# Scaling expert outputs by the gate column directly, and moving the residual sum to the head of VectorE's step, in a gated attention and mixture-of-experts block

## The chip, the cores and the metric

One core of a Trainium2 chip runs the whole block. The metric is the device time of one launch in microseconds (us), the median of several runs. One execution was also taken by the hardware profiler; its trace gives every row shown here. TensorE is written PE (its weight loads PEld), VectorE DVE, ScalarE ACT, GpSimd POOL, and the DMA-issuing SyncE SP.

## The reference, cut to what matters

```python
# x: (128, 64, 128), 16 heads of 64, 8 experts, top 2
x = x + tanh(g_xattn) * xattn(layernorm(x), ctx, ctx, mask, Wq, Wk, Wv, Wo)
# the feed-forward half, on n = 8192 tokens
xf = layernorm(x);  logits = xf @ Wg + bg;  probs = softmax(logits)
w, idx = top_k(probs, 2);  w = w / sum(w)
comb = sum(one_hot(idx, 8) * w[..., None], axis=1)          # (n, 8), two non-zero weights
h = relu(einsum('nd,edh->enh', xf, W1) + b1)
y = einsum('enh,ehd->end', h, W2) + b2
x = x + tanh(g_ffn) * einsum('end,ne->nd', y, comb)
```

Every expert is computed for every token, and the routing weights (zero for six of eight experts) scale its output.

## The kernel before, in words

The 128 sequences of 64 tokens are cut into 16 groups of 8 sequences (512 tokens). Each engine runs one written-out program over 163 steps `s`; a group spans 8 steps, and `i = s % 8` is the place in the group. There is no scheduler: what orders the engines is this list and the semaphores. In one step of the steady state the attention of one sequence is advanced at several stages, two heads of the next group's queries are projected, and one expert is computed for a group that is two groups behind (`FFN_LAG` is 16 steps). Matmuls are done in three half-precision passes (lines L46 to L48), so for each result ScalarE writes a high half and VectorE or GpSimd the low half.

Two of the eight PSUM banks hold scores. The other six are handed out in turn by `take_bank`: each TensorE block takes the next bank and waits until what was in it six takes ago has been read. In a steady step TensorE takes banks for queries, values, queries, transposed probabilities (`PT`, L310), first half of the hidden layer (`hid`), attention output (`PV`), second half of `hid`, in odd steps the output projection `Wo`, and the expert output `y`. So in an even step the first `hid` block takes the bank of the previous step's `Wo` (free when VectorE has made the residual sum, L720), and the `PV` block the bank of the previous `y` (free when VectorE has scaled it, L704). With the router's extra bank taken at i=0, the first `hid` block of i=1 takes the bank of `y`.

VectorE's step in order: scale `y` into `y_scaled` (L704), the low half of the transposed normalised tokens at i=7 (L662), in even steps the residual sum (L720) for one pair of sequences, then other low halves, softmax sums and maxima, and at the end the router's small operations. At i=0 these are L816 to L828 (`logit`, `above`, `same`, `logit_max`, `expo`), at i=1 L831 to L851: `rank`, `picked`, `picked_sum`, `picked_inv`, `weight3` (L845) and `comb` (L851). `weight3` holds the routing weights three times, for the bias matmul; `comb` holds them once, multiplied by `out_scale[:, 1]`, which is tanh of the feed-forward gate over the square of the number by which the weights were enlarged. `y_scaled` is `y * comb`; GpSimd adds it to `x2` (L922), and VectorE does so for the last 14 (L748).

Of the kernel before, what the change touches and what calls it, by code (L numbers as in the profile page):

```python
# [16 lines left out]
P = 128  # L17
# [33 lines left out]
def flamingo_block(nc, x, ctx, mask, g_xattn, g_ffn, Wq, Wk, Wv, Wo, Wg, bg, W1, b1, W2, b2, out):  # L51
    stack = ExitStack()
    with stack:
# [3 lines left out]
        def sem(name):  # L57
            return stack.enter_context(nc.semaphore(name))
# [52 lines left out]
        weight3 = sb("weight3", [P, GT, 3, QUAD])  # L111
        picked_sum = sb("picked_sum", [P, GT])
        picked_inv = sb("picked_inv", [P, GT])
        comb = sb("comb", [P, 2, GT, E])
        pickedT = sb("pickedT", [STACK, N], F16)
        hid = sb("hid", [P, NR, N])
        hidH, hidL = (sb(f"hid{p}", [P, 2, HC, N], F16) for p in "HL")
# [2 lines left out]
        def as_f32(tensor, pattern):  # L120
# [49 lines left out]
        s_marked, s_mask_in = sem("score_banks_marked"), sem("mask_in_bank")  # L170
        s_ln = [{k: sem(f"ln{w}_{k}") for k in ("stats", "aggr", "var", "minus", "shift", "rows")} for w in range(2)]
        s_logit_in, s_gt, s_eq, s_gmax, s_gshift = (sem(n) for n in ("logit_in", "gt", "eq", "gate_max", "gate_shift"))
        s_rank, s_picked, s_psum, s_pinv, s_comb1, s_comb, s_pickT_low = (
            sem(n) for n in ("rank", "picked", "picked_sum", "picked_inv", "comb1", "comb", "pickedT_low"))

        s_zero, s_ident, s_one, s_tri, s_half, s_vzero, s_w3zero, s_b2zero = (
            sem(n) for n in ("ident_zero", "ident", "tri_one", "tri", "minus_half", "v_zero", "weight3_zero", "b2_zero"))
# [81 lines left out]
        def _(pe):  # L259
# [133 lines left out]
            for s in range(FIRST, LAST):  # L393
                g, i = s // GB, s % GB
                sooner = 2 if s < 0 else 0
                eg, ei = (s - FFN_LAG) // GB, (s - FFN_LAG) % GB
                hg, hi = (s - 1 - FFN_LAG) // GB, (s - 1 - FFN_LAG) % GB
                if within(g + 1, GROUPS):
                    queries(g + 1, 2 * i)
                if within(s // 2, TILES):  # L400
                    values(s // 2, s % 2)
                if within(g + 1, GROUPS):
                    queries(g + 1, 2 * i + 1)
                if within(s, B):
                    scores(s)
                if within(s - 2, B):
                    transpose_probs(s - 2)
                if within(eg, GROUPS):
                    hidden(eg, ei, 0)
                if within(s - 3, B):  # L410
                    probs_values(s - 3)
                if within(eg, GROUPS):
                    hidden(eg, ei, 1)
                if s % 2 == 1 and within((s - 5) // 2, TILES):
                    project_out((s - 5) // 2)
                if within(hg, GROUPS):
                    expert_out(hg, hi)
                if i == 6 and within(g + 2, GROUPS):
                    transposes("xT", g + 2, xhat, (s_ln[0]["rows"], g + 3), s_xT)
                if i == 6 - sooner and within(g + 1, GROUPS):  # L420
                    transposes("ctxT", g + 1, ctx_raw[:, (g + 1) % 2], ctx_loaded(g + 1), s_ctxT)
                if i == 6 and within(g - 1, GROUPS):
                    transposes("x2T", g - 1, x2hat, (s_ln[1]["rows"], g), s_x2T)
                if i == 0 and within(g - 2, GROUPS):
                    for freed in take_bank("logit", g - 2):
                        pe.wait_ge(*freed)
                    pe.wait_ge(s_x2T_low, g - 1)
                    for t in range(GT):
                        lhs = [c[:, g % 2, t * P:(t + 1) * P] for c in (x2tH, x2tL)]
                        last = three_passes(pe, bk("logit", g - 2)[:, t * E:(t + 1) * E], lhs, (wgH[:, :], wgL[:, :]))  # L430
                    last.then_inc(s_logit, 1)
                if i == 2 and within(g - 2, GROUPS):
                    for freed in take_bank("pickedT", g - 2):
                        pe.wait_ge(*freed)
                    pe.wait_ge(s_comb1, g - 1)
                    for t in range(GT):
                        last = pe.transpose(bk("pickedT", g - 2)[0:STACK, t * P:(t + 1) * P],
                                            weight3[:, t, :, :].rearrange("p n e -> p (n e)"), ident[:, :])
                    last.then_inc(s_pickT, 1)
                if i == 3 and within(g - 2, GROUPS):  # L440
                    for freed in take_bank("b2 out", g - 2):
                        pe.wait_ge(*freed)
                    pe.wait_ge(s_pickT_low, g - 1)
                    for t in range(GT):
                        cols = slice(t * P, (t + 1) * P)
                        last = pe.matmul(bk("b2 out", g - 2)[:, t * D:(t + 1) * D], pickedT[:, cols], b2_halves[:, :],
                                         start=True, stop=True)
                    last.then_inc(s_b2, 1)
# [185 lines left out]
        def _(dve):  # L634
# [53 lines left out]
            for s in range(FIRST, LAST):  # L688
# [3 lines left out]
                was_sooner = 2 if s - 1 < 0 else 0  # L692
                eg, ei = (s - FFN_LAG) // GB, (s - FFN_LAG) % GB
                yg, yi = (s - 2 - FFN_LAG) // GB, (s - 2 - FFN_LAG) % GB
                if within(yg, GROUPS):
                    m = yg * E + yi
                    if yi == 0:
                        dve.wait_ge(s_comb, yg + 1)
                    if m == 0:
                        dve.wait_ge(s_wdve, H // 4 + 10)  # L700
                    if m >= 2:
                        dve.wait_ge(*y_added(m - 2))
                    dve.wait_ge(s_y, m + 1)
                    dve.tensor_tensor(y_scaled[:, m % 2], bk("y", yg, yi)[:, :].rearrange("p (t d) -> p t d", t=GT),  # L704
                                      comb[:, yg % 2, :, yi].unsqueeze(2).to_broadcast([P, GT, D]),
                                      ALU.mult).then_inc(s_scaled, 1)
                if ph == 6 and within(pg - 1, GROUPS):
                    transposed_low("x2T", pg - 1, x2tL[:, (pg - 1) % 2, :], x2tH[:, (pg - 1) % 2, :], s_x2T_high, s_x2T_low)
                if s % 2 == 0 and within((s - 6) // 2, TILES):
                    t = (s - 6) // 2  # L710
                    rg, ri = t // GT, t % GT
                    if t == 0:
                        dve.wait_ge(s_scale, 1)
                        dve.wait_ge(s_wdve, H // 4 + 10)
                    if ri == 0 and rg >= NX2:
                        dve.wait_ge(s_store[(rg - NX2) % 2], 16 * ((rg - NX2) // 2 + 1))
                    if ri == 0:
                        dve.wait_ge(*x_loaded(rg))
                    dve.wait_ge(s_wo, t + 1)
                    dve.scalar_tensor_tensor(x2[:, rg % NX2, ri, :], bk("Wo", t)[:, 0:D], out_scale[:, 0:1],  # L720
                                             x_raw[:, rg % NX, ri, :], ALU.mult, ALU.add).then_inc(s_res, 1)
                if ph == 6 and within(pg + 2, GROUPS):
                    transposed_low("xT", pg + 2, xtL[:, pg % 2, :], xtH[:, pg % 2, :], s_xT_high, s_xT_low)
                if ph == 6 - was_sooner and within(pg + 1, GROUPS):
# [104 lines left out]
                if i == 1 and within(g - 2, GROUPS):  # L829
                    dve.wait_ge(s_above, g - 1)  # L830
                    dve.tensor_reduce(rank[:, :, :], above[:, :, :, :], AX.X, ALU.add).then_inc(s_rank, 1)  # L831
                    dve.wait_ge(s_rank, g - 1)
                    dve.wait_ge(s_gate_exp, g - 1)
                    if g >= 3:
                        dve.wait_ge(s_pickT, g - 2)
                    dve.scalar_tensor_tensor(picked[:, :, :], rank[:, :, :], 1.5, expo[:, g % 2], ALU.is_lt,
                                             ALU.mult).then_inc(s_picked, 1)
                    dve.wait_ge(s_picked, g - 1)
                    dve.tensor_reduce(picked_sum[:, :], picked[:, :, :], AX.X, ALU.add).then_inc(s_psum, 1)
                    dve.wait_ge(s_psum, g - 1)  # L840
                    dve.reciprocal(picked_inv[:, :], picked_sum[:, :]).then_inc(s_pinv, 1)
                    dve.wait_ge(s_pinv, g - 1)
                    if g == 2:
                        dve.wait_ge(s_w3zero, 1)
                    dve.tensor_tensor(weight3[:, :, :, 0:E], picked[:, :, :].unsqueeze(2).to_broadcast([P, GT, 3, E]),  # L845
                                      picked_inv[:, :].unsqueeze(2).unsqueeze(3).to_broadcast([P, GT, 3, E]),
                                      ALU.mult).then_inc(s_comb1, 1)
                    dve.wait_ge(s_comb1, g - 1)
                    if g >= 4:
                        dve.wait_ge(s_scaled, E * (g - 3))  # L850
                    dve.tensor_scalar(comb[:, g % 2], weight3[:, :, 0, 0:E], out_scale[:, 1:2], None,  # L851
                                      ALU.mult).then_inc(s_comb, 1)
                if i == 2 and within(g - 2, GROUPS):
                    dve.wait_ge(s_pickT_high, g - 1)
# [207 lines left out]
```

## Time and profile before

| | us |
|---|---|
| median of 3 runs (1050.44 to 1051.08) | 1050.65 |
| the profiled execution's own time | 1048.99 |
| its span, first to last instruction | 1047.3 |
| PE busy | 980.3 (94%) |
| ACT busy | 931.9 (89%) |
| DVE busy | 858.6 (82%) |
| POOL busy | 814.6 (78%) |

Busy shares are means over the whole span, and matmuls overlap in the pipe. What sets the time in a stretch is read from who waits for whom there, and from the start-to-start distance of TensorE's blocks.

### The profile page before, as it was taken

To read this page: it belongs to the slowest core of one execution; us is meant where nothing else is said; L and a number is where in the kernel's file an instruction comes from. 1 tells how busy PE (TensorE), PEld (TensorE's weight loads), DVE (VectorE), ACT (ScalarE), POOL (GpSimd) and SP (SyncE) were. 2 spreads that over 40 slices of the span, in tenths; PEclk is the share of its full clock that TensorE was granted. 3 is DMA by queue.
4 is the path that set the end of the run, shared out by engine and by line. 5 is a ranking of instruction groups with operands and counts; after the bars stand their busy time and mean duration, and the time that the engine had idled before them with its cause. 6 is when DMAs were issued, how large, how long until landed. Compare 5 with 4: busy or idle time off the path is not lost.

```text
span 1047.3 us, 36218 instructions
## 1 busy us (share of the span) xinstructions
PE 980.3 (94%) x13749; PEld 730.3 (70%) x13749; DVE 858.6 (82%) x1741; ACT 931.9 (89%) x1793; POOL 814.6 (78%) x817
## 2 busy tenths in 40 slices
PE   6878799999999999999999999999999999999886
PEld 4456567777777777777777777777777777777654
DVE  3587688897988889798888979888897988888777
ACT  3899899999898999989899998989999898989765
POOL 3587768778888877888887788888778888889942
PEclk9999899999999999999999999999999999999999
DMA  9134232323223232322333232232323222222100
GB/s 231 29 55 73 52 59 46 58 47 65 50 42 60 55 58 47 65 50 42 57 57 60 45 65 50 43 60 54 61 44 65 50 32 51 44 42 53 33 2 22
DMA packets 319803, 56.91 MB, mean 54 GB/s; under 512 B 288744, under 2 KB 319504, under 8 KB 319632
## 3 DMA queue, kind: packets, MB, share of 16 engines
q1 hardware_dynamic: 319632, 54.59, 27.9%
q8 instruction: 112, 1.84, 0.7%
q14 instruction: 59, 0.48, 0.2%
HBM read 16.81 MB, written 4.19 MB: 20 GB/s over the span
## 4 chain that ended last, share of the span: by engine, by line
PE 55%; POOL 12%; ACT 12%; DVE 10%; issue 9%; DMA 1%; ACTq 0%; POOLq 0%; SPq 0%; DVEq 0%
PE bank L46 17%; PE bank L48 16%; PE bank L47 16%; POOL hidL L888 3%; POOL rstd L869 3%; PE bank L310 3%; PE bank L265 2%; POOL ptL L927 2%; ACT bank L518 2%; ACT vH L558 2%; ACT pt L578 2%; DVE above L824 2%; DVE comb L851 1%; ACT qH L462 1%; POOL prob L933 1%
## 5 line engine op out<-in xcount | busy, mean ns | idle before, releaser
L888 POOL TENSOR_TENSOR hidL<-hid,hidH 128x512 f16<-128x512 f32 x242 | 277.6, 1163 | 17.6 <-ACT hidH L492 17.6
L927 POOL TENSOR_TENSOR ptL<-pt,ptH 128x512 f16<-128x512 f32 x128 | 149.4, 1167 | 104.7 <-ACT pt L578 104.7
L482 ACT ACTIVATE hid<-bank,b1col 128x512 f32<-128x512 f32 x256 | 189.0, 738 | 8.2 <-PE bank L48 8.1
L492 ACT ACTIVATE hidH<-bank,b1col 128x512 f16<-128x512 f32 x256 | 191.8, 749 | 0.0
L46 PE MATMUL bank<-w2H,hidH 128*128 128x128 f16 x1024 | 178.0, 219 | 13.3 <-POOL hidL L888 7.4
L657 DVE TENSOR_TENSOR qL<-bank,qH 128x512 f16<-128x512 f32 x224 | 153.4, 685 | 40.6 <-ACT qH L462 37.2
L462 ACT ACTIVATE qH<-bank 128x512 f16<-128x512 f32 x256 | 159.3, 626 | 28.2 <-PE bank L48 27.3
L48 PE MATMUL bank<-w2H,hidL 128*128 128x128 f16 x1024 | 178.1, 219 | 0.0
L47 PE MATMUL bank<-w2L,hidH 128*128 128x128 f16 x1024 | 178.1, 219 | 0.0
L922 POOL TENSOR_TENSOR x<-x,y_scaled 128x512 f32<-128x512 f32 x114 | 146.0, 1281 | 12.8 <-DVE x L731 12.8
L933 POOL TENSOR_TENSOR prob<-prob,row_inv 128x512 f32<-128x512 f32 x128 | 133.7, 1044 | 15.5 <-DVE row_inv L767 15.5
L704 DVE TENSOR_TENSOR y_scaled<-bank,comb 128x512 f32<-128x512 f32 x128 | 87.6, 684 | 58.6 <-PE bank L48 57.6
L46 PEld LDWEIGHTS bank<-w2H,hidH 128*128 128x128 f16 x1024 | 100.1, 98 | 27.0 <-issue 19.4
L46 PE MATMUL bank<-x2tH,w1H 128*128 128x512 f16 x256 | 97.4, 381 | 13.4 <-DVE x L720 11.3
L47 PEld LDWEIGHTS bank<-w2L,hidH 128*128 128x128 f16 x1024 | 100.1, 98 | 6.8
L46 PE MATMUL bank<-ctH,qH 128*128 128x64 f16 x1024 | 103.0, 193 | 0.6 <-ACT bank L518 0.6
L46 PEld LDWEIGHTS bank<-ctH,qH 128*128 128x128 f16 x1024 | 92.3, 98 | 16.0 <-ACT bank L518 1.0
L46 PE MATMUL bank<-ptH,vdH 128*128 128x64 f16 x1024 | 103.0, 193 | 0.3 <-issue 0.3
L48 PE MATMUL bank<-ptH,vdL 128*128 128x64 f16 x1024 | 103.2, 193 | 0.0
L47 PE MATMUL bank<-ptL,vdH 128*128 128x64 f16 x1024 | 103.2, 193 | 0.0
L48 PE MATMUL bank<-ctH,qL 128*128 128x64 f16 x1024 | 103.1, 193 | 0.0
L47 PE MATMUL bank<-ctL,qH 128*128 128x64 f16 x1024 | 103.1, 193 | 0.0
(139 smaller groups left out, 3527.3 us busy)
## 6 DMA issues: line engine op xcount, KB each, us to landing
vdH<-vH SPq DMA_DIRECT2D x256, 64.0 KB, 2.3
vdL<-vL SPq DMA_DIRECT2D x256, 64.0 KB, 2.3
x_raw<-in_x SPq DMA_DIRECT2D x16, 256.0 KB, 3.1
ctx_raw<-in_ctx SPq DMA_DIRECT2D x16, 256.0 KB, 3.1
mask_raw<-in_fside_Bx1xSxS SPq DMA_DIRECT2D x32, 128.0 KB, 2.8
out_x<-x SPq DMA_DIRECT2D x16, 256.0 KB, 2.7
qH<-in_L_xattn_Wq SPq DMA_DIRECT2D x1, 512.0 KB, 5.4
qH<-in_L_xattn_Wk SPq DMA_DIRECT2D x1, 512.0 KB, 7.3
```

Of the source, the lines that this page charges most:

```text
L46: e.matmul(dst, lhs[0], rhs[0], start=start, stop=False, skip_group_check=True)
L47: e.matmul(dst, lhs[0], rhs[1], start=False, stop=False, skip_group_check=True)
L48: return e.matmul(dst, lhs[1], rhs[0], start=False, stop=stop, skip_group_check=True)
L462: act.activation(qH[:, g % 2, 2 * j + g2, :, h2, :], bk("Q", g, h)[:, :].rearrange("p (b q) -> p b q", b=GB), ACT.Copy).then_inc(s_q_high, 1)
L482: act.activation(hid[:, k % NR, :], bk("hid", g, e, c)[:, :], ACT.Relu, bias=b1col[:, e, c:c + 1]).then_inc(s_relu[c], 1)
L492: act.activation(hidH[:, m % 2, c, :], bk("hid", g, e, c)[:, :], ACT.Relu, bias=b1col[:, e, c:c + 1]).then_inc(s_hid_high[c], 1)
L657: dve.tensor_tensor(qL[at], bk("Q", g, h)[:, :].rearrange("p (b q) -> p b q", b=GB), qH[at], ALU.subtract).then_inc(s_q_low[h % 2], 1)
L704: dve.tensor_tensor(y_scaled[:, m % 2], bk("y", yg, yi)[:, :].rearrange("p (t d) -> p t d", t=GT), comb[:, yg % 2, :, yi].unsqueeze(2).to_ ...
L888: pool.tensor_tensor(hidL[:, m % 2, c, :], hid[:, k % NR, :], hidH[:, m % 2, c, :], ALU.subtract).then_inc(s_hid_low[c], 1)
L922: pool.tensor_tensor(acc, acc, y_scaled[:, m % 2], ALU.add).then_inc(s_y_add, 1)
L927: pool.tensor_tensor(ptL[:, b % 2, :], pt[:, b % 2, :], ptH[:, b % 2, :], ALU.subtract).then_inc(s_pt_low, 1)
L933: pool.tensor_tensor(p, p, row_inv[:, b % NPB, :].unsqueeze(2).to_broadcast([P, JG, S]), ALU.mult).then_inc(s_normal, 1)
```

## The change

The tile `comb`, its semaphore pair and its instruction L851 go. L704 becomes one instruction of VectorE with a tensor, a per-partition scalar and a second tensor: `y * out_scale[:, 1] * weight3[:, :, 0, e]`. Since `weight3` has one buffer where `comb` had two, its writer waits until the eight `y_scaled` of the group before are done. The block of the residual sum now stands ahead of the block of L704. TensorE's wait for `weight3` has another semaphore name and the same producer.

```diff
-        comb = sb("comb", [P, 2, GT, E])
...
-                    pe.wait_ge(s_comb1, g - 1)
+                    pe.wait_ge(s_comb, g - 1)
...
-                if within(yg, GROUPS):
-                    m = yg * E + yi
-                    if yi == 0:
-                        dve.wait_ge(s_comb, yg + 1)
-                    if m == 0:
-                        dve.wait_ge(s_wdve, H // 4 + 10)
-                    if m >= 2:
-                        dve.wait_ge(*y_added(m - 2))
-                    dve.wait_ge(s_y, m + 1)
-                    dve.tensor_tensor(y_scaled[:, m % 2], bk("y", yg, yi)[:, :].rearrange("p (t d) -> p t d", t=GT),
-                                      comb[:, yg % 2, :, yi].unsqueeze(2).to_broadcast([P, GT, D]),
-                                      ALU.mult).then_inc(s_scaled, 1)
-                if ph == 6 and within(pg - 1, GROUPS):
-                    transposed_low("x2T", pg - 1, ...)
                 if s % 2 == 0 and within((s - 6) // 2, TILES):
...
                     dve.scalar_tensor_tensor(x2[:, rg % NX2, ri, :], bk("Wo", t)[:, 0:D], out_scale[:, 0:1],
                                              x_raw[:, rg % NX, ri, :], ALU.mult, ALU.add).then_inc(s_res, 1)
+                if within(yg, GROUPS):
+                    m = yg * E + yi
+                    if yi == 0:
+                        dve.wait_ge(s_comb, yg + 1)
...
+                    dve.wait_ge(s_y, m + 1)
+                    dve.scalar_tensor_tensor(y_scaled[:, m % 2], bk("y", yg, yi)[:, :].rearrange("p (t d) -> p t d", t=GT),
+                                             out_scale[:, 1:2], weight3[:, :, 0, yi].unsqueeze(2).to_broadcast([P, GT, D]),
+                                             ALU.mult, ALU.mult).then_inc(s_scaled, 1)
+                if ph == 6 and within(pg - 1, GROUPS):
+                    transposed_low("x2T", pg - 1, ...)
...
+                    if g >= 3:
+                        dve.wait_ge(s_scaled, E * (g - 2))
                     dve.tensor_tensor(weight3[:, :, :, 0:E], ...
-                                      ALU.mult).then_inc(s_comb1, 1)
-                    dve.wait_ge(s_comb1, g - 1)
-                    if g >= 4:
-                        dve.wait_ge(s_scaled, E * (g - 3))
-                    dve.tensor_scalar(comb[:, g % 2], weight3[:, :, 0, 0:E], out_scale[:, 1:2], None,
                                       ALU.mult).then_inc(s_comb, 1)
```

## Rows read from the trace of the kernel before

**Rows 1.** Engines' busy time (instructions) over one steady group, 640 to 701 us

```profile
640.00:701.00 61.00, 59.71 (x856) 44.78 (x856) 52.35 (x109) 56.45 (x110) 49.87 (x51) 1.00 0.29 54
```

**Rows 2.** TensorE's waits, whole span: us in total, times, longest

```profile
PE bank L46 <- DVE x L720: 11.3, 14, 1.2
```

**Rows 3.** The weight loads' waits, whole span: same columns

```profile
PEld bank L46 <- DVE y_scaled L704: 6.0, 15, 1.0
```

**Rows 4.** The chain that ended last, around 640 us: start, us, what

```profile
637.94 0.72 DVE weight L845
...
638.68 1.03 DVE comb L851
...
640.35 0.35 DVE x L720
...
640.74 0.39 PE bank L46
```

**Rows 5.** TensorE in order of time: start, us, instruction, idle before

```profile
152.05 0.39 PE L46 MATMUL bank<-x2tH,w1H 128*128 128x512 f16 x1 [1.14 <-DVE x L720]
...
631.28 0.63 PE L310 MATMUL bank<-ident,prob 128*128 128x128 f32 x4
632.04 0.39 PE L46 MATMUL bank<-x2tH,w1H 128*128 128x512 f16 x1
...
639.36 0.63 PE L310 MATMUL bank<-ident,prob 128*128 128x128 f32 x4
640.74 0.39 PE L46 MATMUL bank<-x2tH,w1H 128*128 128x512 f16 x1 [0.75 <-DVE x L720]
...
647.17 0.64 PE L310 MATMUL bank<-ident,prob 128*128 128x128 f32 x4
647.64 0.38 PE L46 MATMUL bank<-x2tH,w1H 128*128 128x512 f16 x1
...
943.15 0.39 PE L46 MATMUL bank<-x2tH,w1H 128*128 128x512 f16 x1 [1.21 <-DVE x L720]
```

**Rows 6.** VectorE in order of time

```profile
631.30 0.68 DVE L704 TENSOR_TENSOR y_scaled<-bank,comb 128x512 f32<-128x512 f32 x1
...
639.74 0.69 DVE L704 TENSOR_TENSOR y_scaled<-bank,comb 128x512 f32<-128x512 f32 x1
640.35 0.34 DVE L720 SCALAR_TENSOR_TENSOR x<-bank,out_scale,x_raw 128x128 f32<-128x128 f32 x1
```

**Rows 7.** GpSimd in order of time

```profile
637.38 2.29 POOL L888 TENSOR_TENSOR hidL<-hid,hidH 128x512 f16<-128x512 f32 x2
639.63 1.26 POOL L922 TENSOR_TENSOR x<-x,y_scaled 128x512 f32<-128x512 f32 x1
```

**Rows 8.** ScalarE in order of time

```profile
641.60 0.69 ACT L482 ACTIVATE hid<-bank,b1col 128x512 f32<-128x512 f32 x1 [0.21 <-PE bank L48]
...
653.39 0.60 ACT L462 ACTIVATE qH<-bank 128x512 f16<-128x512 f32 x1 [1.47 <-PE bank L48]
```

**Rows 9.** Groups of VectorE's instructions by line: busy, mean ns, idle before

```profile
L637 DVE SCALAR_TENSOR_TENSOR aL<-bank,aH 128x512 f16<-128x512 f32 x4 | 2.8, 692 | 7.4 <-ACT aH L525 7.4
```

**Rows 10.** Durations by line, ns min/median/max, first and last start

```profile
L704 DVE TENSOR_TENSOR y_scaled<-bank,comb x128: 656/691/694, 151.0 to 1042.5; 128x512 f32<-128x512 f32 x128
L851 DVE TENSOR_SCALAR comb<-weight,out_scale x16: 242/1024/1027, 150.0 to 1024.0; 128x32 f32<-128x32 f32 x16
L731 DVE SCALAR_TENSOR_TENSOR x<-bank,out_scale,x x16: 734/742/743, 164.8 to 1029.7; 128x512 f32<-128x512 f32 x16
L720 DVE SCALAR_TENSOR_TENSOR x<-bank,out_scale,x_raw x64: 336/342/351, 74.1 to 998.8; 128x128 f32<-128x128 f32 x64
L824 DVE TENSOR_TENSOR above<-logit x16: 426/1140/2320, 140.4 to 1017.2; 128x256 f32<-128x256 f32 x16
```

**Rows 11.** The chain that ended last, from 985 us on

```profile
985.02 0.69 DVE y_scaled L704
...
1024.03 0.25 DVE comb L851
...
1042.54 0.06 DVE y_scaled L704
```

More of the change, by code:

```diff
@@ L172, in flamingo_block @@
         s_logit_in, s_gt, s_eq, s_gmax, s_gshift = (sem(n) for n in ("logit_in", "gt", "eq", "gate_max", "gate_shift"))
-        s_rank, s_picked, s_psum, s_pinv, s_comb1, s_comb, s_pickT_low = (
-            sem(n) for n in ("rank", "picked", "picked_sum", "picked_inv", "comb1", "comb", "pickedT_low"))
+        s_rank, s_picked, s_psum, s_pinv, s_comb, s_pickT_low = (
+            sem(n) for n in ("rank", "picked", "picked_sum", "picked_inv", "comb", "pickedT_low"))
         s_zero, s_ident, s_one, s_tri, s_half, s_vzero, s_w3zero, s_b2zero = (
@@ L694, in _ @@
                 yg, yi = (s - 2 - FFN_LAG) // GB, (s - 2 - FFN_LAG) % GB
-                if within(yg, GROUPS):
-                    m = yg * E + yi
-                    if yi == 0:
-                        dve.wait_ge(s_comb, yg + 1)
-                    if m == 0:
-                        dve.wait_ge(s_wdve, H // 4 + 10)
-                    if m >= 2:
-                        dve.wait_ge(*y_added(m - 2))
-                    dve.wait_ge(s_y, m + 1)
-                    dve.tensor_tensor(y_scaled[:, m % 2], bk("y", yg, yi)[:, :].rearrange("p (t d) -> p t d", t=GT),
-                                      comb[:, yg % 2, :, yi].unsqueeze(2).to_broadcast([P, GT, D]),
-                                      ALU.mult).then_inc(s_scaled, 1)
-                if ph == 6 and within(pg - 1, GROUPS):
-                    transposed_low("x2T", pg - 1, x2tL[:, (pg - 1) % 2, :], x2tH[:, (pg - 1) % 2, :], s_x2T_high, s_x2T_low)
                 if s % 2 == 0 and within((s - 6) // 2, TILES):
@@ L721, in _ @@
                                              x_raw[:, rg % NX, ri, :], ALU.mult, ALU.add).then_inc(s_res, 1)
+                if within(yg, GROUPS):
+                    m = yg * E + yi
+                    if yi == 0:
+                        dve.wait_ge(s_comb, yg + 1)
+                    if m == 0:
+                        dve.wait_ge(s_wdve, H // 4 + 10)
+                    if m >= 2:
+                        dve.wait_ge(*y_added(m - 2))
+                    dve.wait_ge(s_y, m + 1)
[3 more added lines that the diff above has]
+                if ph == 6 and within(pg - 1, GROUPS):
+                    transposed_low("x2T", pg - 1, x2tL[:, (pg - 1) % 2, :], x2tH[:, (pg - 1) % 2, :], s_x2T_high, s_x2T_low)
                 if ph == 6 and within(pg + 2, GROUPS):
```

## Prediction

> **What bounds the kernel now.** I read the busy table by stretch first. In a steady group of about 61 us TensorE is busy for 59.7 us, ScalarE for 56.5, VectorE for 52.4 and GpSimd for 49.9 [rows 1]. So TensorE sets the pace, all others have slack on average, and a gain can only come from TensorE's few idle moments. The list of TensorE's waits names them, and the largest one that comes back in every group is the wait for the residual sum L720: 14 times, 11.3 us [rows 2]. One list further, the weight loads wait 15 times, 6.0 us, for the scaled expert output L704 [rows 3].
>
> The profile counts an idle time from a modelled end of the matmul before, so I take the cost of a stall from start-to-start distances. Four transposes L310 and the hidden layer's first matmul behind them stand 0.47 us apart where nothing is waited for (647.17 to 647.64). At i=2 they stand 1.38 us apart (639.36 to 640.74): the stall is 0.91 us, where the bracket says 0.75, so a bracket lacks 0.16. At i=1 they stand 0.76 us apart (631.28 to 632.04): 0.29 us [rows 5].
>
> Then I read the chain of waits back from the stall at 640.74. It runs from TensorE into L720, behind it L704, behind it `comb` for 1.03 us, behind it `weight3` and the rest of the router on VectorE [rows 4]. VectorE is late there because the router's eleven small operations at i=0 and i=1 pile up, not because its whole group is full. Every group between 211 and 884 us repeats this to within 0.02 us: 12 stalls of 0.91 us. The first is 1.14 and the last 1.21 by the bracket, so 1.30 and 1.37 [rows 5]. Sum: 12 x 0.91 + 1.30 + 1.37 = 13.6 us. That is the pot.
>
> **The change, part by part.**
>
> *L851 is removed.* In the stalled step it costs 1.03 us plus 0.03 between instructions, from the end of `weight3` at 638.66 to the start of L704 at 639.74: 1.08 us [rows 4, 6]. Its shortest instance is 242 ns and the median 1024 [rows 10]: in the steady group it ends at 639.71, with GpSimd's second L888 (637.38 + 2.29 = 639.67) [rows 7]. It is held, and the whole of it goes, hold included.
>
> *L720 stands ahead of L704.* L720 starts 0.61 us after L704 [rows 6]; so it comes another 0.61 us earlier, 1.69 us in all. It would start at 638.66 and end at about 639.03, and with the 0.04 us that TensorE took to react (640.70 to 640.74, [rows 4]) release the bank at 639.07. TensorE is ready at 639.36 + 0.47 = 639.83. The whole stall goes, with 0.76 us to spare; either of the two edits alone would take most of it. In the first and last of the 14 TensorE is ready 1.30 and 1.37 us before the old release, also under 1.69. The wait for Wo that L720 brings in front of L704 costs nothing: TensorE issues the projection before the expert output which L704 needs. In steps where VectorE waits for `y`, L720 now fills part of that wait. At i=7, where L704 moves past nothing but keeps its place ahead of the x2T low half, there is no residual sum, since i=7 is odd. No DMA is issued in a moved block; the store that L720 waits for is issued three steps before.
>
> *What is late next, once TensorE is 0.91 us earlier.* First L704, for the PV bank: it would run from about 638.92 to 639.66, and TensorE wants it one hidden block (0.65 us) after 639.83, at 640.48: 0.8 us spare. Then ScalarE: it was only 0.21 us idle before it took the hidden layer at 641.60, so it follows by 0.2 us at once and lags by 0.7 us. But before 653.39 it is idle for 1.47 us waiting for TensorE [rows 8], so it makes up the lag within a step or so, as no TensorE block in between is handed a bank by ScalarE with less than that to spare. From 653.39 on everything (ScalarE, GpSimd's layer-norm work, the small stall at i=5) hangs from TensorE and shifts whole. So the price of this item is the pot, -13.6 us.
>
> *L704 takes a scalar from memory as well.* A three-operand instruction from a bank with a constant takes 692 ns (L637) [rows 9], no more than L704's 691; with a per-partition scalar, L731 takes 742 [rows 10]. So 51 ns more for L704, 128 times 6.5 us of VectorE's time. VectorE has 8.6 us idle in a group (61.0 - 52.35, [rows 1]), loses 8 x 0.05 = 0.4 us and gets 1.0 us back. It is paid only where TensorE waits for L704: the 0.29 us stall at i=1, where the start at 631.30 is followed by TensorE's at 632.04 [rows 5, 6]. The waits for L704 number 15 [rows 3], two of them in the end part and 13 at this place: 13 x 0.051 = +0.7 us. Bounds for the term: nothing (an immediate costs nothing) and, above, what an operation that GpSimd holds costs, below. I take the 51 ns, because L731 is the same form from the same banks.
>
> *Added waits.* The writer of `weight3` waits for the eighth `y_scaled` of the group before, which VectorE itself issued at the head of the same step, some 7 us earlier: nothing. The strided column of `weight3` replaces the strided column of `comb`, both broadcast: nothing, bounded by L731's 743 ns, whose second tensor is read in full.
>
> *The end part.* From 985 us on L704 stands in the chain five times by name, first at 985.02, last at 1042.54; `comb` once, 0.25 us [rows 11]. 5 x 0.051 = 0.25 us against 0.25: zero, with perhaps 1.5 us either way, since there VectorE's two-input operations and GpSimd's hold each other by chance of phase.
>
> Whether the new L704 can be held by GpSimd is the one point on which a rule bears. L720 at 640.35 takes two operands from SBUF beside its bank (the scalar and x_raw) and ran for 0.34 us wholly inside GpSimd's L922 (639.63 to 640.89); its 64 instances span 336 to 351 ns, and L731's 16 span 734 to 743 [rows 6, 7, 10]. So the form is never held. The Trainium skill, page "SBUF — State Buffer", section "Who interferes with whom", says that a DVE instruction with two SBUF inputs contends with a GpSimd instruction that reads SBUF; were the scalar an input in that sense, the new L704 would be held, and the sum would be that of the third rival instead of this one. By the rows it is not.
>
> **The sum.** -13.6 + 0.7 + 0 = -12.9 us: the profiled execution's span goes from 1047.3 to 1034.4 and its own time from 1048.99 to 1036.1. The median of the runs stands 1.66 above that execution: 1050.65 - 12.9 = 1037.8 us.
>
> **Rivals.**
>
> 1. *The hold is inherited.* What is removed is a hold by GpSimd until 639.67; if L720 were held in its place, it would end at 639.67 + 0.35 + 0.04 = 640.06, and 0.23 us of the 0.91 stay: 14 x 0.23 = 3.2 us less, 1041.0. For it: L851's end. Against it: L720 unheld under L922.
> 2. *ScalarE becomes what TensorE waits for.* If only the 0.21 us by which ScalarE was idle is gained, 14 x 0.21 = 2.9, less 0.7: 1048.4. For it: 56.45 of 61 us busy and back to back at i=1 and i=2. Against it: 1.47 us idle soon after.
> 3. *The new L704 is held by GpSimd.* At i=1 it would be longer by what L824's median is above its minimum, 0.71 us [rows 10]: 13 x (0.71 + 0.05) = 9.9; -13.6 + 9.9 = -3.7: 1046.9.
> 4. *Slower: the same hold, but long.* L824 at its longest is held for 1.89 us. From a mean hold of 1.0 us at i=1 on (13 x 1.05 = 13.6) the pot is spent; at 1.89 it is 13 x 1.94 = 25.2, so +11.6: 1062.3. The narrow spread of L731 speaks against it.
> 5. *No change:* a stall of equal size opens later in the group, so that the period stays 61.1 us: 1050.6. Only the POOL wait of i=5 is a candidate, and its chain starts from TensorE.
>
> **How the numbers follow.** Forecast 0.75; rival 1 0.09; rival 2 0.06; rival 3 0.04; rival 4 0.02; rival 5 0.04. The forecast's own range, from the end part (1.5 us either way) and the 0.7 us term (zero to double), is 1036.0 to 1039.8. The range is 1035.8 to 1041.6: it takes in rival 1 and leaves out the rest, about 0.18. About 0.2% (2.1 us) is what a measurement of this kernel can tell from no change. Faster is the forecast with rivals 1 and 3 and most of 2: 0.93. Same is rival 5 and a little of 2: 0.05. Slower is rival 4: 0.02.
>
> **What would show it.** Right: no wait of TensorE for L720 left (14 before); start-to-start 0.47 us from L310 to the hidden block at i=2; a period of about 60.2 us instead of 61.1; L704 at 742 ns; the i=1 distance at 0.81 us. Wrong, and telling which: L720 longer than 351 ns (rival 1), a new wait of TensorE for ScalarE between i=2 and i=4 (rival 2), L704 instances above 800 ns (rivals 3 and 4), an i=5 distance that grew (rival 5).

## Result, and the profile after

| | before | after |
|---|---|---|
| median, us (runs) | 1050.87 (4) | 1036.55 (4) |
| ratio, 95% interval | | 0.9866 [0.9849, 0.9884] |
| the same, on another chip in 5 rounds | 1049.32 (11) | 1037.93 (6) |
| ratio, 95% interval | | 0.9885 [0.9865, 0.9905] |
| span of the profiled execution | 1047.3 | 1036.5 |

The change makes the kernel 14.3 us faster by the first measurement (1050.87 less 1036.55). By the second it is 12.1 us, which is 1049.32 times the ratio's distance from 1, 0.0115. The forecast was 12.9 us. The two intervals overlap between 0.9865 and 0.9884, and 12.9 us (0.9877) lies in it.

The list of TensorE's waits in the changed kernel (us in total, times, longest) answers to [rows 2], and the list of the weight loads' waits to [rows 3]. First TensorE:

```profile
PE bank L46 <- POOL hidL L884: 7.5, 14, 1.7
...
PE bank L46 <- DVE y_scaled L716: 3.0, 14, 0.5
```

then the weight loads:

```profile
PEld bank L46 <- DVE y_scaled L716: 9.1, 16, 2.2
```

The wait for the residual sum, which was TensorE's largest in total, is gone from the list, all 14 of them. The wait for the scaled output has grown a little past the point from which the profile counts it for TensorE too.

Three engines in order of time show where it went. TensorE, answering to [rows 5]:

```profile
625.06 0.63 PE L309 MATMUL bank<-ident,prob 128*128 128x128 f32 x4
625.88 0.39 PE L46 MATMUL bank<-x2tH,w1H 128*128 128x512 f16 x1 [0.18 <-DVE y_scaled L716]
...
633.20 0.63 PE L309 MATMUL bank<-ident,prob 128*128 128x128 f32 x4
633.67 0.38 PE L46 MATMUL bank<-x2tH,w1H 128*128 128x512 f16 x1
```

VectorE, answering to [rows 6]:

```profile
631.72 0.71 DVE L846 TENSOR_TENSOR weight<-picked,picked_inv 128x96 f32<-128x96 f32 x1
632.36 0.34 DVE L705 SCALAR_TENSOR_TENSOR x<-bank,out_scale,x_raw 128x128 f32<-128x128 f32 x1
632.62 0.73 DVE L716 SCALAR_TENSOR_TENSOR y_scaled<-bank,out_scale,weight 128x512 f32<-128x512 f32 x1
```

and GpSimd, answering to [rows 7]:

```profile
631.16 2.29 POOL L884 TENSOR_TENSOR hidL<-hid,hidH 128x512 f16<-128x512 f32 x2
633.42 1.26 POOL L918 TENSOR_TENSOR x<-x,y_scaled 128x512 f32<-128x512 f32 x1
```

At i=2 the distance from the transposes to the hidden block is 0.47 us: nothing is waited for. The residual sum (now L705) ends at 632.70, 0.97 us before TensorE wants the bank. It and the new L716 ran while GpSimd's L884 was under way (to 633.45), for 0.34 and 0.73 us: no hold. At i=1 the distance is 0.82 us, so that stall grew from 0.29 to 0.35.

The durations of the new instruction (ns min/median/max) answer to the first row of [rows 10]:

```profile
L716 DVE SCALAR_TENSOR_TENSOR y_scaled<-bank,out_scale,weight x128: 718/746/753, 151.2 to 1031.7; 128x512 f32<-128x512 f32 x128
```

The span of the profiled execution moved by less than the medians, by 10.8 us. To find out why, take two moments that both traces have: the end of TensorE's first stall at i=5 (177.32 before, 177.09 after) and the last transposes of x2hat (the normalised rows that go into the feed-forward half). The latter are shown here for the kernel before in order of time

```profile
1008.81 0.61 PE L265 MATMUL bank<-ident,x2hat 128*128 128x128 f32 x4
```

and for the changed one,

```profile
996.90 0.60 PE L264 MATMUL bank<-ident,x2hat 128*128 128x128 f32 x4
```

Between the two moments lie 831.49 and 819.81 us, 11.7 us less, and the first L720 stall (1.3 us) lies ahead of the first moment: 13.0 us. The rest is TensorE's clock. The table by stretch (us, busy time of PE, PEld, DVE, ACT, POOL, granted clock of TensorE, DMA share, GB/s) of the kernel before

```profile
0.00:140.00 140.00, 107.92 (x1256) 75.07 (x1257) 89.78 (x186) 112.85 (x225) 88.57 (x96) 0.96 0.42 88
...
1022.00:1028.00 6.00, 5.06 (x63) 4.00 (x64) 5.73 (x13) 4.75 (x9) 2.31 (x2) 1.00 0.15 44
```

and of the changed one

```profile
0.00:140.00 140.00, 109.35 (x1240) 75.72 (x1241) 88.69 (x185) 112.10 (x222) 87.54 (x95) 0.94 0.42 88
...
1010.00:1016.00 6.00, 5.29 (x45) 3.57 (x46) 5.76 (x12) 3.81 (x8) 1.16 (x1) 0.72 0.16 46
```

show a granted clock of 0.94 against 0.96 in the start, ahead of the first new L716 (151.2), and of 0.72 against 1.00 near the end. The changed kernel arrived 1.1 us late at 177 (177.09, where 177.32 less 1.3 would be 176.0) and took 39.6 instead of 38.5 us behind 997. In the later profile of the same kernel (e10 below) the last transposes of x2hat and the clock near the end are

```profile
997.21 0.61 PE L264 MATMUL bank<-ident,x2hat 128*128 128x128 f32 x4
```

```profile
1010.00:1016.00 6.00, 4.89 (x61) 3.82 (x62) 5.76 (x12) 4.89 (x9) 1.91 (x2) 1.00 0.15 44
```

and the end stretch takes 38.5 us of its span of 1035.7. The start had the clock of the kernel before, 0.96, in e7, which contains the change. So neither belongs to the change; it is the spread of single executions, which in the kernel before reached from 1045.2 to 1050.3 us of span on one chip.

### The profile page after: what moved, and what is told of

It is laid out like the page before. It is cut to its first block, busy times and chain, and to the rows that moved or that the text cites. A ratio compares the mean times of both kernels' runs of the same rounds, so it can differ in the third digit from the quotient of the medians.

```text
span 1036.5 us, 36203 instructions
## 1 busy us (share of the span) xinstructions
PE 981.6 (95%) x13749; PEld 732.9 (71%) x13749; DVE 852.1 (82%) x1725; ACT 925.5 (89%) x1793; POOL 814.9 (79%) x817
## 4 chain that ended last, share of the span: by engine, by line
PE 65%; POOL 14%; ACT 7%; issue 7%; DVE 5%; DMA 1%; POOLq 0%; ACTq 0%; SPq 0%; DVEq 0%
PE bank L46 19%; PE bank L48 19%; PE bank L47 19%; POOL hidL L884 4%; PE bank L309 4%; POOL rstd L865 3%; POOL ptL L923 2%; PE bank L264 2%; DVE above L823 2%; POOL prob L929 1%; ACT qH L461 1%; ACT bank L517 1%; DVE y_scaled L716 1%; ACT vH L557 1%; POOL qL L877 1%
## 5 line engine op out<-in xcount | busy, mean ns | idle before, releaser
L884 POOL TENSOR_TENSOR hidL<-hid,hidH 128x512 f16<-128x512 f32 x242 | 277.7, 1163 | 18.5 <-ACT hidH L491 18.4
L716 DVE SCALAR_TENSOR_TENSOR y_scaled<-bank,out_scale,weight 128x512 f32<-128x512 f32 x128 | 95.1, 743 | 35.4 <-PE bank L48 34.9
L46 PE MATMUL bank<-xtH,aH 128*128 128x512 f16 x256 | 98.6, 385 | 5.7 <-DVE qL L656 2.8
```

The costliest lines, as they stand in the source:

```text
L46: e.matmul(dst, lhs[0], rhs[0], start=start, stop=False, skip_group_check=True)
L716: dve.scalar_tensor_tensor(y_scaled[:, m % 2], bk("y", yg, yi)[:, :].rearrange("p (t d) -> p t d", t=GT), out_scale[:, 1:2], weight3[:, :, ...
L884: pool.tensor_tensor(hidL[:, m % 2, c, :], hid[:, k % NR, :], hidH[:, m % 2, c, :], ALU.subtract).then_inc(s_hid_low[c], 1)
```

## Experiments

The table has, for each kernel, the length of a regular group (the distance between the x2hat transposes of successive groups), and the stalls of TensorE in it: at i=1 and i=2 as distance less 0.47 us, at i=5 whether the idle time of 0.40 to 0.42 us that the profile prints in brackets is there. Each ratio is against the kernel before on the same chip.

| kernel | group, us | i=1 | i=2 | i=5 | median | ratio, 95% interval |
|---|---|---|---|---|---|---|
| before | 61.09 | 0.29 | 0.91 | yes | 1050.87 | |
| changed | 60.23 | 0.35 | 0 | yes | 1036.55 | 0.9866 [0.9849, 0.9884] |
| e1, order only | 60.34 | 0.28 | 0.18 | yes | 1039.61 | 0.9910 [0.9888, 0.9931] |
| e2, removal only | 60.21 | 0.34 | 0 | yes | 1039.39 | 0.9905 [0.9874, 0.9935] |
| e3, comb not held | 60.22 | 0.28 | 0.07 | yes | 1038.73 | 0.9906 [0.9884, 0.9928] |
| e4, no scalar | 60.15 | 0.28 | 0 | yes | 1034.88 | 0.9873 [0.9855, 0.9891] |
| e5, y scaled early | 59.86 | 0 | 0 | yes | 1032.64 | 0.9839 [0.9824, 0.9853] |
| e6, comb twice | 63.11 | 0.28 | 2.13 | yes | 1076.32 | 1.0256 [1.0241, 1.0271] |
| e7, hidL early | 60.21 | 0.34 | 0 | no | 1035.37 | 0.9864 [0.9847, 0.9880] |
| e8, both | 59.86 | 0 | 0 | no | 1032.62 | 0.9838 [0.9823, 0.9852] |
| e9, e5 with sooner norm | 59.87 | 0 | 0 | no | 1033.13 | 0.9848 [0.9825, 0.9870] |
| e10, changed again | 60.23 | 0.34 | 0 | yes | 1037.93 | 0.9885 [0.9865, 0.9905] |

The medians scatter by 1 to 3 us, in part with the clock granted in the start; a group's length repeats to about 0.01 us inside one profile and between the two profiles of the changed kernel, and is what I go by.

### e1: the move alone

The block of the residual sum is put ahead of the scaling of `y`; `comb` stays.

```diff
+                if s % 2 == 0 and within((s - 6) // 2, TILES):   # the residual sum, first
+                    ...
                 if within(yg, GROUPS):                            # y * comb, as before
```

> The kernel before, with the residual sum moved ahead of the scaling of y and nothing else. My theory: the residual sum comes 0.61 us earlier at i=2, TensorE is ready 0.91 us before the old release, so 0.30 us of the stall stay in each group: 14 x 0.61 = 8.5 us faster than before, about 1042.4. The router's multiplication by the gate stays at 1.02 us. Rival (the move alone is enough, since what is held is not on the path): 12.9 us faster, 1038. Rival (ScalarE takes over): at most 3 us faster, 1048.

Measured: 0.18 us of the stall stay, not 0.30, and the group is 0.75 us shorter. VectorE in order of time shows why:

```profile
634.09 1.03 DVE L851 TENSOR_SCALAR comb<-weight,out_scale 128x32 f32<-128x32 f32 x1
635.03 0.34 DVE L706 SCALAR_TENSOR_TENSOR x<-bank,out_scale,x_raw 128x128 f32<-128x128 f32 x1
635.29 0.68 DVE L717 TENSOR_TENSOR y_scaled<-bank,comb 128x512 f32<-128x512 f32 x1
```

The residual sum does not read `comb`. It starts at 635.03, 0.09 us before `comb` ends; L704 in [rows 6], which waits for `comb`, started 0.03 behind its end. The independent instruction saves that 0.12 us as well. Counted by the stalls, the move alone is worth 14 times 0.73, some 10 us of the 13, not 8.5; by the ratio it is 9.4 us.

### e2: the removal alone

The changed kernel, with the residual sum put back behind L716 (the diff above, reversed).

> The changed kernel with the residual sum put back behind the scaling of y. My theory: the residual sum starts at 638.66 + 0.66 = 639.32 and releases the bank at 639.71, TensorE is ready at 639.83: in the 12 regular groups nothing is left of the stall. In the first and the last 1.30 and 1.37 less 1.03 remain, 0.6 us in all. Gain 13.6 - 0.6 - 0.7 = 12.3 us, about 1038.6: the removal alone is worth nearly the whole, and the move about 0.6 us on top of it, though alone it is worth 8.5. Rival (the two edits add up): removal alone is worth 12.9 - 8.5 = 4.4 us, 1046.5.

As expected, nothing is left at i=2 in the regular groups, and the group is as short as with both edits (60.21 and 60.23). In the first and the last 0.31 and 0.33 us remain (forecast 0.27 and 0.34). So once `comb` is gone the move has one use, those two places. The measured ratio, with an interval of 0.6%, cannot tell the two kernels apart. The rival by which the parts add up is out: counted in the traces they are 10 and 12.4 us alone and 13 together, and the ratio of e2 (10.0 us, at least 6.8 by its interval) excludes the 4.4 us that it needed.

### e3: is comb work or a hold?

```diff
-                    dve.tensor_scalar(comb[:, g % 2], weight3[:, :, 0, 0:E], out_scale[:, 1:2], None,
-                                      ALU.mult).then_inc(s_comb, 1)
+                    dve.tensor_reduce(comb[:, g % 2], weight3[:, :, 0, 0:E].unsqueeze(3), AX.X, ALU.max).then_inc(s_comb, 1)
```

> The kernel before, with comb written by a reduction over an axis of length one in place of the multiplication; the factor tanh(gate) over the square of the weights' enlargement is left out, so the output is not scaled by it. Same place, same 128x32 written, same waits. My theory: the 1.02 us is a hold by GpSimd and not work; a reduction reads one operand and is not held. It takes about 0.2 us, everything behind it comes 0.84 us earlier, 0.07 us of the stall stay in a regular group and 0.46 and 0.53 in the first and last: 14 x 0.84 = 11.8 us faster, about 1039.1. Rival (the 1.02 us is what any write and read of that tile costs): 1050.9, instruction about 1.0 us.

The kernel leaves the factor out, so it is a measurement and not a substitute. The durations of the new L851 (ns min/median/max), to be read beside L851 in [rows 10]:

```profile
L851 DVE TENSOR_REDUCE comb<-weight x16: 185/186/188, 152.3 to 1014.3; 128x32 f32<-128x32 f32 x16
```

All 16 take 0.19 us, in the same place with the same 32 elements per partition, and 0.07 us of the stall stay, as forecast. So `comb`'s 1.02 us were for the most part GpSimd's hold and not work: 0.84 us go with an instruction of another form, and the multiplication's own shortest instance, 0.24 us [rows 10], puts the hold at 0.78. The group is as short as the changed kernel's (60.22 and 60.23): the gain comes from getting rid of the hold, whichever way. A kernel that also applies the factor by an unheld instruction was not run.

### e4: the price of the scalar

```diff
-                    dve.scalar_tensor_tensor(y_scaled[...], bk("y", yg, yi)[...], out_scale[:, 1:2], weight3[...], ALU.mult, ALU.mult)
+                    dve.tensor_tensor(y_scaled[...], bk("y", yg, yi)[...], weight3[...], ALU.mult)
```

> The changed kernel with the per-partition scalar of the scaling of y left out (two operands again, the factor tanh(gate) over the square of the weights' enlargement is missing in the output). My theory: the instruction takes 691 ns in place of 743, the stall at i=1 is 0.29 us again in place of 0.34: 13 x 0.05 = 0.7 us less, and up to 0.3 us less in the end part, so about 1035.7 against 1036.6. Rival (the added operand costs VectorE alone): no difference to the changed kernel, distance at i=1 stays 0.81 us.

This kernel, too, leaves the factor out. The instruction's median is 684 ns against 746 in the changed kernel. The stall at i=1 is 0.28 us again, and the rival by which the operand costs VectorE alone is out: TensorE pays for it at i=1. The distance there is 0.75 us, against 0.82 in the changed kernel and 0.81 in e2, which has the scalar as well. That is 0.06 to 0.07 us, 0.8 to 0.9 us over 13 groups, where the forecast had 0.7. The group is 0.09 us shorter than the changed kernel's before rounding, a little more than that. The other 0.02 stand at i=5, where TensorE's idle time is 0.42 us in the first two profiles and 0.40 to 0.41 in e1 to e6 and e10, with and without the scalar, so they are not its price.

### e5: the other stall on VectorE

The distance at i=1 is a wait for L716, which the router's five operations at the end of i=0 push back. Here that one instruction goes ahead of them.

```diff
-                if within(yg, GROUPS):
+                if within(yg, GROUPS) and i != 1:
                     scale_output(yg, yi)
...
+                if i == 0 and within(g - 3, GROUPS):
+                    scale_output(g - 3, E - 1)
                 if i == 0 and within(g - 2, GROUPS):
                     l, m, e_ = logit[:, g % 2], ...            # the router
```

> The changed kernel with one more move: the scaling of y that stands at the head of step i=1 is issued at the end of step i=0, ahead of the router's five operations. My theory: TensorE's stall of 0.35 us at i=1 is the wait for that instruction, which the router's operations delay by 2.5 us. Moved, it fills the 0.55 us in which VectorE waits for the logits and pushes them by 0.3 us; the long operation behind them is held by GpSimd until the same moment anyway. Stall gone, 13 x 0.35 = 4.5 us less than the changed kernel, about 1032. Rival (the router's chain is pushed whole, ScalarE's exponential and all behind it come 0.3 us later, and TensorE meets a new wait at i=2): no gain, 1036.5.

VectorE in order of time:

```profile
620.26 0.75 DVE L672 SCALAR_TENSOR_TENSOR y_scaled<-bank,out_scale,weight 128x512 f32<-128x512 f32 x1 [0.34 <-PE bank L48]
620.92 0.18 DVE L820 SCALAR_TENSOR_TENSOR logit<-bank,bgrow 128x32 f32<-128x32 f32 x1
621.14 0.69 DVE L828 TENSOR_TENSOR above<-logit 128x256 f32<-128x256 f32 x1
```

It fills the wait for the logits, and `above`, started later, takes 0.69 us in place of the 1.14 that is usual [rows 10]. Both end 0.28 us behind the end of the GpSimd instruction that was under way (L889, to 621.55, here; L888, to 629.91, before): the hold ends when GpSimd is done, whenever one starts. The stall is gone and the group is 0.37 us shorter, which makes 4.6 us up to the last x2hat transposes. The end gives 0.6 of it back: behind them this kernel takes 39.1 us where e10 took 38.5, both at clock 1.00 there, and TensorE's longest wait for VectorE's `hidL` is 2.8 in place of 2.0 us. What is left is some 4 us. The ratio is 0.9839, 16.9 us less than the kernel before on that chip (1049.13). Against the changed kernel's two measurements, the interval lies wholly below that of the second (from 0.9865) and overlaps a little with that of the first (from 0.9849), so the shorter group carries the verdict.

### e6: comb twice

```diff
+                    dve.tensor_scalar(comb2[:, g % 2], weight3[:, :, 0, 0:E], out_scale[:, 1:2], None, ALU.mult)
                     dve.tensor_scalar(comb[:, g % 2], weight3[:, :, 0, 0:E], out_scale[:, 1:2], None, ALU.mult)
```

> The kernel before, with the multiplication of the routing weights by the gate done twice, the first into a tile that nobody reads. My theory: what this instruction costs is set by GpSimd's instruction that runs at that moment. The first of the two is held to the end of GpSimd's hidL as before (1.02 us). The second either gets in at once (0.24 us: 14 x 0.27 = 3.8 us slower than before) or is held to the end of the next one, GpSimd's sum of x and y_scaled, 1.2 us more: 14 x 1.2 = 17 us slower. Since TensorE is already waiting there, each addition is paid in full. Rival (the price is the instruction's own): 1.05 us more for each, 14.7 us slower, both instances at 1.02 us.

The two instructions, ns min/median/max:

```profile
L853 DVE TENSOR_SCALAR comb<-weight,out_scale x16: 241/1024/1031, 149.6 to 1051.3; 128x32 f32<-128x32 f32 x16
L855 DVE TENSOR_SCALAR comb<-weight,out_scale x16: 228/1306/1315, 150.5 to 1051.4; 128x32 f32<-128x32 f32 x16
```

The same work takes 1024 and 1306 ns. VectorE and then GpSimd in one group:

```profile
654.27 1.31 DVE L855 TENSOR_SCALAR comb<-weight,out_scale 128x32 f32<-128x32 f32 x1
655.62 0.69 DVE L706 TENSOR_TENSOR y_scaled<-bank,comb 128x512 f32<-128x512 f32 x1
```

```profile
654.28 1.26 POOL L926 TENSOR_TENSOR x<-x,y_scaled 128x512 f32<-128x512 f32 x1
```

The second is held to the end of the next GpSimd operation (655.54), as one branch of the theory had it, and the stall grows by 1.22 us. The rival (equal price) is out. But the kernel lost 27 us, not 17: a group grew by 2.02 us. What came on top is TensorE's clock. The table by stretch of this kernel:

```profile
205.00:270.00 65.00, 62.52 (x882) 46.71 (x879) 54.75 (x111) 57.66 (x112) 50.97 (x52) 0.97 0.27 51
270.00:330.00 60.00, 57.64 (x828) 43.45 (x825) 51.57 (x107) 54.19 (x106) 47.62 (x49) 1.00 0.30 55
...
215.00:217.00 2.00, 2.00 (x24) 1.18 (x21) 2.00 (x5) 1.65 (x3) 0.00 (x0) 0.52 0.04 8
217.00:219.00 2.00, 2.00 (x25) 1.99 (x24) 1.33 (x4) 1.41 (x3) 1.81 (x2) 0.63 0.37 58
```

In the group around 211 us the clock fell to about its lower level (0.52 of full speed; the level is 1.2 of 2.4 GHz) behind the stall that ended at 214.08; in the next group, with an equal stall, it did not. The groups are 63.92 and 62.28 us long by turns, 1.64 us apart.

### e7 to e9: the stall at i=5

At i=5 TensorE waits for GpSimd's low half of a hidden block, which stands behind 4 us of layer-norm operations. e7 and e8 issue it ahead of them, on the changed kernel and on e5.

```diff
+                if i == 4 and within(m, TAIL):
+                    hidden_low(m, 1)                            # and no longer at the head of i == 5
                 if within(g + 2, GROUPS) and i == 4 - sooner:
                     ln_scale_shift(0, g + 2)
```

> The changed kernel with one move on GpSimd: the low half of the second hidden block at i=5 is made at the end of step i=4, ahead of the layer-norm operations (about 4 us) instead of behind them. My theory: TensorE's other regular stall, 0.42 us by the bracket at i=5, waits for that low half; it is worth 13 x 0.58 = 7.5 us, about 1029. Rival: the layer-norm's scale and shift come 1.1 us later, ScalarE's normalised rows and TensorE's transposes at i=6 wait for them and the gain is given back: 1036.5 or slower.

> The changed kernel with both moves. My theory: the two stalls lie apart in the group and add up: 4.5 + 7.5 = 12 us less than the changed kernel, about 1024.5, with no regular wait of TensorE left. Rival: with TensorE never waiting, ScalarE (56.5 us busy of 61) or VectorE gets behind it and a new wait opens: less than either move's sum, 1028 or more.

The stall at i=5 is gone, and the group is practically as long as without the move (60.21 against 60.23; with e5's move 59.86 both times). The rival's number was right and its reason wrong. TensorE in order of time, then ScalarE, of e7:

```profile
665.36 0.60 PE L264 MATMUL bank<-ident,ctx_raw 128*128 128x128 f32 x4
666.32 0.63 PE L264 MATMUL bank<-ident,x2hat 128*128 128x128 f32 x4 [0.36 <-issue]
```

```profile
659.44 1.67 ACT L505 ACTIVATE x2hat<-x,shift,rstd 128x128 f32<-128x128 f32 x4
660.98 0.62 ACT L461 ACTIVATE qH<-bank 128x512 f16<-128x512 f32 x1
...
665.44 0.78 ACT L491 ACTIVATE hidH<-bank,b1col 128x512 f16<-128x512 f32 x1
```

ScalarE normalised the rows at 659.44 without waiting; that was not late. TensorE's x2hat block takes the bank of the hidden block whose high half ScalarE finishes at 666.22, and starts 0.10 us behind that. It stands 0.96 us behind the block before it, where it is 0.44 in the changed kernel. From 652.18 to 675 us ScalarE has no gap, and 0.52 of the 0.58 us won at i=5 are waited for here. e9 puts it to the test: the statistics and GpSimd's operations for the other layer-norm come one step sooner, so that nothing is late at i=5 and no norm either.

```diff
-                    if i == 3 - sooner:
+                    if i == (1 if sooner else 2):
                         ln_stats(0, g + 2, ...)                 # ln_aggr and GpSimd's part likewise
```

> The kernel of the early scaling (one move more than the changed kernel) with the layer-norm statistics of x, and GpSimd's operations on them, one step sooner (i=2 and 3 in place of 3 and 4), so that only the other layer-norm stands ahead of the low half at i=5. My theory after the run of the GpSimd move: the stall at i=5 is covered by ScalarE, which runs back to back from i=4 to i=7; TensorE gains 0.58 us at i=5 and waits as long at i=6, where its third transpose block takes the bank that ScalarE's hidH must free. So no gain: group of 59.9 us as with the early scaling alone, about 1032. Rival (what I had written for the move on GpSimd: the late layer-norm gives it back): here the layer-norm is not late, so the gain stays, 13 x 0.58 = 7.5 us less, about 1025.

59.87 us in a group, no gain over e5. TensorE's waits of e9:

```profile
PE bank L264 <- issue: 10.4, 14, 3.1
```

Two of the 14, 5.9 us together, lie in the start, ahead of 127 us. The other 12 are one in each group. TensorE in order of time, then ScalarE:

```profile
662.77 0.60 PE L264 MATMUL bank<-ident,ctx_raw 128*128 128x128 f32 x4
663.75 0.63 PE L264 MATMUL bank<-ident,x2hat 128*128 128x128 f32 x4 [0.38 <-issue]
```

```profile
662.87 0.78 ACT L491 ACTIVATE hidH<-bank,b1col 128x512 f16<-128x512 f32 x1
```

The distance is 0.98 us, 0.54 more than in the changed kernel, and the block again starts 0.10 us behind the end of ScalarE's high half (663.65). That ScalarE is the limit there rests on e7's rows and on two different removals that both gained nothing; a kernel with less work for ScalarE in that stretch was not run.

### e10: the changed kernel again

> The changed kernel once more, beside the kernel before on one chip, in five rounds, to narrow the interval: the two traces differ by 0.86 us in each regular group and by 12.9 us between the first and the last stall, so 12.5 to 13 us and a ratio of 0.988. The first measurement (ratio 0.9866) had 14.3 us, of which 1.5 us would be chance.

0.9885 [0.9865, 0.9905], a group of 60.23 us.

## Why the prediction was right

*The bound and the pot.* 13.6 us were to be had from 14 waits for the residual sum, priced by start-to-start distances. All 14 went. By the idle times that the profile prints in brackets alone (11.3 us) the pot would have come out 2.3 us too small.

*Removal of comb, 1.08 us, hold included.* Right: e3 shows that 0.84 us go without the removal once the form is not held, e6 that the length follows GpSimd's instruction of the moment.

*The move, 0.61 us.* Right in kind, 0.12 us too small (e1): I let the residual sum start behind the end of `weight3`, and it started 0.07 us before it. The residual sum ends 0.97 us before TensorE wants the bank; with the 0.04 us of reaction that the forecast counted it is 0.93, where I had 0.76. (My own terms, 638.66 + 0.35 + 0.04, would have made that 0.78; nothing hangs on it.) That "either of the two edits alone would take most of it" holds: 10 and 12.4 of 13.0 us.

*What is late next.* Nothing was, in the group: its length fell by 0.86 us, which is 0.91 less the 0.06 by which the stall at i=1 grew, within rounding. ScalarE made up its lag, but not where I said. One row of the kernel before (its hidden block at 640.74), then two of the changed one (hidden block at 633.67):

```profile
645.37 0.60 ACT L462 ACTIVATE qH<-bank 128x512 f16<-128x512 f32 x1
```

```profile
638.29 0.60 ACT L461 ACTIVATE qH<-bank 128x512 f16<-128x512 f32 x1
646.31 0.60 ACT L461 ACTIVATE qH<-bank 128x512 f16<-128x512 f32 x1 [1.46 <-PE bank L48]
```

This instruction starts 4.63 and 4.62 us behind the hidden block: the lag was gone by then, made up in small gaps, and the 1.47 us that I counted on were not touched (1.46). I had also sized the lag by a bracket. By starts ScalarE lost 0.41 us before the hidden layer (640.71 to 641.60, where 0.48 is usual) and not 0.21, so it lagged by 0.5 us and not 0.7. The step held with more room than argued, and the argument for it was a weak one.

*The scalar.* Forecast +0.7 us; by e4 it is 0.8 to 0.9, since the instruction grew by 55 to 62 ns and not by 51 (746 against 691 before and 684 in e4). The distance at i=1 is 0.82 us, forecast 0.81.

*Added waits.* Nothing was forecast, and nothing shows in the regular group: `weight3` (L846) starts at 631.72, 0.03 us behind `picked_inv`, as in the kernel before.

*The form is not held.* Right: 718 to 753 ns for 128 instances of the new L716, and 332 to 352 ns for the 64 of the residual sum (L705). The rule of the Trainium skill that was weighed (page "SBUF — State Buffer", section "Who interferes with whom") has a DVE instruction with two SBUF inputs contend with a GpSimd instruction that reads SBUF. The traces fit it if a per-partition scalar in SBUF is not counted as such an input: L716, with a scalar and one tensor there, ran unheld beside GpSimd's L884. Rival 1 falls with L705, rivals 3 and 4 with L716.

*The end part.* Zero was forecast, give or take 1.5 us. In e10, where the clock held, it took 38.5 us behind the last x2hat transposes, as before. In the first profile of the changed kernel the clock fell there and it took 1.1 us more.

*Rivals 2 and 5.* ScalarE did not become what TensorE waits for with this change, and no new stall opened. e7 and e9 show that ScalarE does become it once the stall at i=5 is taken away, at another place.

*The number.* The mechanism and the sum came out; that the median did as well (1036.55, forecast 1037.8) is in part luck, since medians of one kernel differ by 1 to 3 us and the two measurements gave 14.3 and 12.1 us. The span of the profiled execution was forecast at 1034.4 and was 1036.5: that miss is the clock in the start and near the end, to which the forecast gave no term. The forecast's own range, too, was added up narrowly: 1.5 and 0.7 us either way make 1035.6 to 1040.0, not 1036.0 to 1039.8.

## What to carry to other kernels

Price a stall from start-to-start distances, and look at what the late engine did just before: an operation of 0.24 us there cost 1.02 us because another engine held it. Issuing the instruction that frees the bank sooner and shortening the chain ahead of it overlap in what they gain; count the time to the moment at which the waiting engine is ready, not the sum of the parts. Once one engine runs a stretch without a gap, taking away the other engine's stall in that stretch only moves it.

## What the runs showed of the hardware beyond that

- In these traces two VectorE instructions in a row overlap by 0.07 to 0.09 us where the second does not wait for the first (632.36 against an end at 632.43; 635.03 against 635.12); where it does, it starts 0.03 us behind the end (`comb` and L704 before).
- The identical small multiplication took 241, 1024 or 1306 ns, by what GpSimd was doing; a reduction in its place took 185 to 188 in all 16 instances.
- A stall can cost more than itself, but need not: in every other group of e6 TensorE's granted clock fell to 0.52 for some 3 us behind a wait of 1.97 us, and the group took 1.6 us more. The changed kernel's first profile has the same at 1010 to 1016 us, behind a wait of 1.98 us, where it cost about 1.1 us. It did not happen behind the equal wait in e10, nor behind 2.04 us in the kernel before, nor behind 2.80 us in e5. What decides it is not shown.
